# In-place scans in PSUM, and a new split of the products by B and C between VectorE, GpSimd and ScalarE

## The reference, cut to what matters

```
dA = exp(delta[:, :, None] * A)                       # decay of each state
h  = dA * h + (delta * u)[:, :, None] * B[:, None, :] # one step per token
y  = einsum('bdn,bn->bd', h, C)                       # sum over the 16 states
```

## Time and profile before

| | us |
|---|---|
| three runs | 2012.32, 2012.53, 2015.65 (median 2012.53) |
| the profiled execution | 2010.69 (its span 2009.1) |
| up to the first scan | 44.2 |
| the 32 steps of scans | 44.2 to 1575.1 |
| the expert part behind them | 434.0 |
| one step in the middle | 47.63 |

### The profile page before, as it was taken

How to read it: one execution, slowest core, us unless ns; L and a number is a source line. 1 busy time by engine, 2 the same in 40 slices (tenths; PEclk the granted TensorE clock), 3 DMA queues, 4 the chain that set the end, 5 groups by cost and what they waited for, 6 DMA issues and landing times. The chain is left out here.

```text
span 2009.1 us, 30384 instructions
## 1 busy us (share of the span) xinstructions
PE 1811.3 (90%) x10816; PEld 1139.7 (57%) x10816; DVE 1807.3 (90%) x1728; ACT 1628.5 (81%) x2957; POOL 1445.0 (72%) x1364
## 2 busy tenths in 40 slices
PE   6899999998988888998999999998986899999998
PEld 2444444444444444444444444444443699999997
DVE  3999999999999999999999999999999977777775
ACT  5999999999999999999999999999997434333332
POOL 2899999999999999999999999999999200000000
PEclk9999999999999999999999999999998999999999
DMA  8433333434343534433333333343435000000000
GB/s 266 95 77 95 77 95 78 109 84 101 88 106 80 115 81 94 95 77 95 77 95 77 95 78 96 85 107 78 107 65 155 1 12 12 12 11 12 6 4 9
DMA packets 79750, 155.88 MB, mean 78 GB/s; under 512 B 12016, under 2 KB 30064, under 8 KB 74992
## 3 DMA queue, kind: packets, MB, share of 16 engines
q1 hardware_dynamic: 73200, 135.52, 28.3%
q10 hardware_dynamic: 6400, 18.42, 3.0%
HBM read 128.86 MB, written 23.99 MB: 76 GB/s over the span
## 5 line engine op out<-in xcount | busy, mean ns | idle before, releaser
L801 DVE TENSOR_TENSOR_SCAN scan<-decay,dbu_ps 128x1024 f32<-128x1024 f32 x512 | 1146.3, 2268 | 64.5 <-issue 53.1
L463 POOL TENSOR_TENSOR scan<-scan,c_rep 128x1024 f32<-128x1024 f32 x255 | 692.7, 2716 | 104.1 <-DVE scan L801 104.1
L1026 PEld LDWEIGHTS dbu_ps<-ident,scan 128*128 128x128 f32 x4096 | 455.3, 141 | 437.6 <-DVE scan L801 208.0
L548 ACT ACTIVATE decay<-d_rep,a_cur 128x510 f32<-128x510 f32 x1024 | 664.7, 709 | 24.1 <-ACT dbc L572 12.0
L1026 PE MATMUL dbu_ps<-ident,scan 128*128 128x128 f32 x4096 | 552.0, 278 | 143.7 <-DVE scan L801 121.7
L457 POOL TENSOR_SCALAR scan<-du_t,b_t 128x256 f32<-128x256 f32 x896 | 561.6, 642 | 0.0
L616 ACT ACTIVATE scan<-du_t,b_t 128x256 f32<-128x256 f32 x1024 | 445.5, 494 | 2.6
L810 DVE TENSOR_TENSOR scan<-scan,c_rep 128x1024 f32<-128x1024 f32 x257 | 327.5, 1275 | 0.0
L740 ACT ACTIVATE decay<-dbu_ps 128x512 f32<-128x512 f32 x256 | 147.9, 597 | 203.2 <-PE dbu_ps L1225 182.8
L1011 PE MATMUL y_ps<-scan,sel 128*32 128x512 f32 x2048 | 274.7, 609 | 0.0
L1039 PE MATMUL pre_ps<-xn,w_pre 128*128 128x512 f32 x512 | 247.2, 606 | 5.0 <-DVE w_pre L790 5.0
(11 more groups left out here) (102 smaller groups left out, 1400.8 us busy)
## 6 DMA issues: line engine op xcount, KB each, us to landing
d_rep<-delta_rows SPq DMA_DIRECT2D x248, 256.0 KB, 5.9
c_rep<-c_rows SPq DMA_DIRECT2D x128, 256.0 KB, 4.5
delta_rows<-delta SPq DMA_DIRECT2D x62, 256.0 KB, 2.2
w_pre<-prepared_weights ACTq DMA_DIRECT2D x15, 866.0 KB, 4.4
prepared_weights<-scan SPq DMA_DIRECT2D x3, 1122.0 KB, 12.8
scan<-in_conv_w SPq DMA_DIRECT2D x4, 512.0 KB, 4.9
w_out<-prepared_weights SPq DMA_DIRECT2D x16, 128.0 KB, 2.1
sp_e<-in_x_rows SPq DMA_DIRECT2D x8, 256.0 KB, 3.5
```

The source lines that it names most:

```text
L463: nc.gpsimd.tensor_tensor(ring[slot % RING], ring[slot % RING], c_rep[par][:, slot // PRS, :].unsqueeze(1).broadcast_to([128, 2, TG]), ALU ...
L548: last = nc.scalar.activation(decay[slot % DEC][:, u, :, 1:], src[:, :, 1:], ACT.Exp, scale=a_cur[:, b, m:m + 1])
L801: nc.vector.tensor_tensor_scan(ring[slot % RING].rearrange("p u t -> p (u t)"), decay[slot % DEC].rearrange("p u a t -> p (u a t)"), dbu_p ...
L1026: last = nc.tensor.transpose(dbu_ps[slot % 2][:, u, 128 * j:128 * j + 128], dbu_t[m % 2][:, j, b, :, :].rearrange("p q c -> p (q c)"), ide ...
```

## The change

Four edits, all in the scan steps.

- DVE's products by C are those of slots 0, 2, 4, 6, 10, 12 and 14 (`DVE_C`, seven instead of eight); POOL makes the other nine, slot 8 now among them.
- For those seven slots the scan writes its states over its own input, in the PSUM buffer `dbu_ps[0]`. The product by C then follows directly behind its own scan, reads the states from PSUM and `c_rep` from SBUF, and writes the ring. The wait for the ring's slot (`quad_done`) moves from the scan to the product.
- `to_channels` of the slot two further on therefore waits for the product (`hc_dve`) where it waited for the scan.
- POOL makes nine of the sixteen products by B of a block and ACT seven. All of POOL's are the form with a column operand now.

PE's order is the same; the transposes of the even slot wait for DVE's product instead of its scan. The core of the diff (the rest renames counts in waits of SP and ACT in the same way):

```diff
-POOL_OUTER = Q * POOL_J
-ACT_OUTER = Q * (JT - POOL_J)
-SHARE = (0, 2, 5, 8)
-FIRST = (0, 3, 6, 8)
-POOL_SHARE = (0, 2, 3, 4, 4)
-POOL_FIRST = (0, 0, 2, 3, 4)
+OUTERS = [(n // 2, n % 2) for n in range(2 * Q)] + [(n // 2, 2 + n % 2) for n in range(2 * Q)]
+POOL_OUTER = 9
+ACT_OUTER = Q * JT - POOL_OUTER
+SHARE = (0, 2, 4, 7)
+FIRST = (0, 3, 5, 7)
+POOL_SHARE = (0, 4, 6, 9, 9)
+POOL_FIRST = (0, 0, 4, 7, 9)
+DVE_C = (0, 2, 4, 6, 10, 12, 14)
+POOL_C = tuple(slot for slot in range(SLOTS) if slot not in DVE_C)
...
+        def c_dve(s, slot):
+
+            return len(DVE_C) * s + sum(x <= slot for x in DVE_C)
...
-                    elif slot % 2 == 0 and slot and has(s, 0):
+                    elif slot and slot - 1 in POOL_C and has(s, 0):
                         times_c(s, i, par, slot - 1)
...
-                if slot % 2 == 0:
+                if slot % 2 == 0 and slot not in DVE_C:
                     wait(dve, quad_done, SLOTS // 2 * s + (slot - RING) // 2 + 1)
...
+                inputs = dbu_ps[slot % 2][:, :, :].rearrange("p u t -> p (u t)")
+                states = inputs if slot in DVE_C else ring[slot % RING].rearrange("p u t -> p (u t)")
+                nc.vector.tensor_tensor_scan(states, decay[slot % DEC].rearrange("p u a t -> p (u a t)"),
+                                             inputs, 0.0, ALU.mult, ALU.add).then_inc(scan_done, 1)
...
+                if slot % 2 == 0:
+                    wait(dve, quad_done, SLOTS // 2 * s + (slot - RING) // 2 + 1)
                 dve.wait_ge(scan_done, SLOTS * s + slot + 1)
-                nc.vector.tensor_tensor(ring[slot % RING], ring[slot % RING],
+                states = dbu_ps[0][:, :, :] if slot in DVE_C else ring[slot % RING]
+                nc.vector.tensor_tensor(ring[slot % RING], states,
...
-                        if slot % 2:
-                            times_c(s, i, par, slot - 1)
+                        if slot in DVE_C:
+                            times_c(s, i, par, slot)
...
-                wait(pe, scan_done, SLOTS * s + slot - 1)
+                if (slot - 2) % SLOTS in DVE_C:
+                    wait(pe, hc_dve, c_dve(s, slot - 2))
+                else:
+                    wait(pe, scan_done, SLOTS * s + slot - 1)
...
-                        pe.wait_ge(scan_done, SLOTS * STEPS - 1 + c // 2)
+                        if c == 0:
+                            pe.wait_ge(hc_dve, c_dve(STEPS - 1, SLOTS - 1))
+                        else:
+                            pe.wait_ge(scan_done, SLOTS * STEPS)
```

More of the change, by code:

```diff
@@ L34 @@
 SZ = 3
-POOL_J = 2
 EPS = 1e-5
@@ L286, in windows, with c_pool @@
                 window(s, s // 2, s % 2)
+        def c_dve(s, slot):
+            return len(DVE_C) * s + sum(x <= slot for x in DVE_C)
+        def c_pool(s, slot):
+            return len(POOL_C) * s + sum(x <= slot for x in POOL_C)
         def is_last(s):
@@ L386, in window @@
                     sp.wait_ge(skip_done, STEPS)
-                    sp.wait_ge(hc_dve, SLOTS // 2 * (STEPS - 1))
-                    sp.wait_ge(hc_pool, SLOTS // 2 * (STEPS - 1))
+                    sp.wait_ge(hc_dve, c_dve(STEPS - 2, SLOTS - 1))
+                    sp.wait_ge(hc_pool, c_pool(STEPS - 2, SLOTS - 1))
                     for e in range(EXPERTS):
@@ L448, in outer @@
                         pool.wait_ge(made_stored[m], 16 if m else 2 * 16)
[L449 to L457, removed]
+                for q, j in OUTERS[first:last]:
+                    nc.gpsimd.tensor_scalar(dbu_t[m % 2][:, j, :, q, :],
+                                            du_t[par][:, j, :].rearrange("p (b c) -> p b c", b=UNITS),
+                                            b_t[par][:, j, q * M + m:q * M + m + 1], 1.0, ALU.mult, ALU.mult)\
+                        .then_inc(dbut_pool, 1)
             def times_c(s, i, par, slot):
@@ L573, in copy_dbc @@
                 act.wait_ge(dbc_ready, s + 1)
-                wait(act, hc_dve, SLOTS // 2 * (s - 1))
-                wait(act, hc_pool, SLOTS // 2 * (s - 1))
+                wait(act, hc_dve, c_dve(s - 2, SLOTS - 1))
+                wait(act, hc_pool, c_pool(s - 2, SLOTS - 1))
                 act.dma_start(c_dram[par, :, :], dbc[RANK + NS:NBC, :]).then_inc(c_stored, 16)
@@ L613, in outer @@
                         act.wait_ge(made_stored[m], 16 if m else 2 * 16)
-                for n in range(first, last):
-                    q, j = n // (JT - POOL_J), POOL_J + n % (JT - POOL_J)
+                for q, j in OUTERS[POOL_OUTER + first:POOL_OUTER + last]:
                     nc.scalar.activation(dbu_t[m % 2][:, j, :, q, :],
@@ L794, in scan @@
             def scan(s, slot):
-                if isinstance(s, int) and s == 0 and slot in (0, RING // 2):
+                if s == 0 and slot in (0, RING // 2):
                     dve.wait_ge(made_stored[2 + slot // (RING // 2)], 16)
@@ L1006, in quad @@
                 extra = 1 if is_last(s) and m == M - 1 and k == KT - 1 else 0
-                pe.wait_ge(hc_dve, SLOTS // 2 * s + 2 * m + k + 1 + extra)
-                pe.wait_ge(hc_pool, SLOTS // 2 * s + 2 * m + k + 1 - extra)
+                wait(pe, hc_dve, c_dve(s, PRS * m + 2 * k + 1) + extra)
+                wait(pe, hc_pool, c_pool(s, PRS * m + 2 * k + 1) - extra)
                 for j in range(Q):
```

## The result

The changed kernel takes 2019.73 us (median of nine runs), the kernel before 2013.46 in the nine runs made beside it. One run of the changed kernel was disturbed (4383.7 us, at a granted clock of 0.443) and is left out of the ratio, which is 1.0029 with a 95% interval from 1.0018 to 1.0039: about 5.8 us slower. The forecast was 2015, 4.3 slower than the profiled execution before.

The account below looks back on a forecast made before the run. It took ACT as late first before the change, then PE and DVE in one ring; 31 steps x 0.12 = 3.7, with up to 1.3 at the end, on 2010.69 gave 2015.0 us, range 1989 to 2040.

Parts of the forecast that it names:

- the hold-up: DVE products with both inputs in SBUF delay POOL's products by C and B: 2.8 and 4.6 us a step.
- PE's windows: PE's work between transposes, at slots 7 to 10 and 14 to 2, delays scans: stalls of 0.79 and 0.58 us.
- POOL: POOL's work falls from 44.84 to 41.7 us a step; with 3.3 of waits, 45.0 fits.
- DVE's own sum: Product 8 and the hold-up go, 0.15 us is added per product: falls by 0.7 to about 45.1 a step.
- First place, slots 7 to 10: PE's work lets scan 10 start no earlier than 6.45 us after scan 7; DVE wants 5.66, stall 0.79.
- Second place, slots 14 to 2: PE's unbroken work puts scan 2 13.97 us after product 12; DVE needs 13.39, stall 0.58.
- The step: From the end of scan 7 to the next scan 7: 47.75 us against 47.63, +0.12.
- in the ring: Closed chain through PE and DVE; five in-place scans and five products lie outside the stall, +-0.8 us a step.
- PSUM: In-place scan stays at 2.268 us and the product reading PSUM takes 1.225.
- PSUM dearer: Slower rival: PSUM access adds 0.037 to 0.08 us to ten DVE instructions, 2026 to 2040 us; chance 0.13.
- POOL not freed: Rival: any DVE product reading `c_rep` holds POOL up, 51.5 us a step, 2130 in all; chance 0.04.
- In-place pair without the 0.15: Faster rival: DVE's product follows its scan without that cost, 47.0 us a step, 1991 or 2001; chance 0.30.

Follow-up runs that it names:

- experiment 5: The changed kernel with the product by C asking for its own scan first and the ring's slot second: 2007.41 us, ratio 0.9978.
- Experiments 1: The changed kernel with PE's output projection behind the transposes of slot 10 instead of ahead of them: 2001.19 us, ratio 0.9948.
- 6: The changed kernel with the products by B back at eight for GpSimd and eight for ScalarE: 2020.73 us, ratio 1.0046.
- 7: The changed kernel with slot 8 also scanned in place and multiplied by C on VectorE: 2047.97 us, ratio 1.0174.
- Experiment 2: The changed kernel with PE's last two sums of the step before placed behind the projection z: 2007.78 us, ratio 0.9983.
- experiment 8: The changed kernel with all scans writing the ring in SBUF again, new product order and shares kept: 2125.15 us, ratio 1.0561.
- experiments 3: The changed kernel with both PE edits, output projection behind slot 10's transposes and last two sums behind z: 2016.59 us, ratio 1.0030.
- 4: The kernel before with both PE edits, output projection behind slot 10's transposes and last two sums behind z: 2077.43 us, ratio 1.0322.
- 9: The changed kernel with the output projection later, the product's waits swapped, and SP's output-weight load behind the delta loads: 1989.57 us, ratio 0.9890.
- 10: The edits of 9 on the changed kernel, plus z directly behind slot 2's transposes and dbc directly behind slot 4's: 1954.78 us, ratio 0.9715.

## Why the prediction was right

The forecast's mechanism held: the hold-up goes, and PE's windows give the gain back. Some of its terms were off and cancel. Point by point:

- **POOL.** Forecast 41.7 a step, measured 41.26. That it would fit was right.
- **DVE's own sum.** Forecast 45.1, and DVE is busy 45.10; but these are unlike things. The forecast counts seven gaps of 0.04 behind scans, and busy time holds no gaps. With the gaps as measured (0.76 a step) the sum is 45.86. The term that was off is the gap: 0.104 and not 0.04, by the order of the waits (experiment 5). The forecast of the step does not rest on this sum, but it has the same gap in it.
- **First place, slots 7 to 10.** Forecast scan 10 at 6.45 behind scan 7 and a stall of 0.79; measured 6.13 and 0.64 (0.56 idle and 0.08 of lost overlap). The forecast took the 5.25 of the earlier trace rows for PE's own work. It was not: in the kernel before the transposes of slot 10 start 0.06 behind the end of scan 8 in every step, as those of slot 9 start 0.05 behind scan 7, so 0.24 of it was a wait for scan 8. In the changed kernel, where scan 8 ends 1.67 before them, the same work of PE takes 5.01. Experiments 1, 6 and 7 show the place: opening it gives 0.68, four more products on ACT do nothing, and product 8 costs only what the stall does not cover.
- **Second place, slots 14 to 2.** Forecast stall 0.58, measured 0.34. Experiment 2 opens it and gives 0.36.
- **The step.** Forecast 47.75, measured 47.79; the shorter windows (scan 10 by 0.32, and scan 2 13.89 behind product 12 instead of 13.97, together -0.4) and the longer gaps (+0.35 in the ring, by experiment 5) nearly cancel, so the agreement is partly luck.
- **PSUM.** The product at 1.225 is as forecast, and the in-place scan costs the same as one into the ring. By the fixed parts of the Trainium skill (VectorE: DVE Perf Modes, "The TRN2 errata") the product would have been some 0.065 dearer, an estimate; the trace does not agree: 1.225 with an input in PSUM, and 1.224 at the least with both in SBUF (experiment 8).
- **The total.** 31 x 0.16 = 5.0 is most of the 5.8 between the runs. The spans of the two profiled executions lie further apart, 2018.2 - 2009.1 = 9.1, and the other 4 us lie in the first and last steps: the second step took 49.37 with PE's clock at 0.93 in the mean (47.64 at 1.00 before), and the last full step 47.79 where it took 46.68. The forecast had only up to 1.3 for the end and nothing for the start. Why the clock fell was not tried, so that the total came within 2 us of the forecast says less than the step does.
- **The rivals.** PSUM dearer: no. POOL not freed: no. In-place pair without the 0.15: no, the product starts 0.104 behind its scan; but experiment 5 shows that 0.07 of this is the order of the waits.

What the prediction did not see: that PE's order has a second side. ACT waits for PE at z and dbc, and PE for ACT at the silu; the forecasts of experiments 3 and 4 failed on it, and from 9 to 10 it was worth 46.90 - 45.72 = 1.18 a step.

## What to carry to other kernels

When two engines hold each other up with operations that have all their inputs in SBUF, as GpSimd's product (2.37 alone, 3.25 behind DVE's) and DVE's did here, take an input of one of them out of SBUF; but look at what the buffer that now holds it was feeding. A buffer held for one instruction longer is a window taken from the engine that refills it, and here, with four engines around nine tenths busy, the gain of one was lost in such windows until the order of that engine was changed too. Look at each wait of the new kernel for what stands ahead of the waited-for work in its engine's order: orders alone, with no work changed, brought 2019.73 - 1954.78 = 65 us here (63 by the ratios to the kernel before), eleven times what the change had cost.

## What was not expected of the hardware

- A DVE product with both inputs in SBUF and a GpSimd operation hold up whichever comes second: GpSimd's product by C goes from 2.37 to 3.25 (the kernel before), DVE's product from 1.22 to 3.45 (experiment 8). With one input in PSUM DVE's product takes 1.225 and GpSimd's 2.367, whoever is first.
- With two waits on DVE's product, the one asked for first stands on the product and the other, in the trace, on a wait instruction (EVENT_SEMAPHORE, 0.021 us) ahead of it. If that is the late one, it costs 0.07 us (0.104 against 0.034) between two dependent operations.
- A scan of 128 x 1024 takes 2.277 us into its own PSUM input and 2.276 into SBUF.
